# Last head's score bounds and causal mask accumulated by TensorE, with small jobs spaced wider and the transposes of two tiles re-placed, in an eight-core transformer layer

## What is computed

```
h   = layernorm(x)
q,k,v = h @ q_w.T, h @ k_w.T, h @ v_w.T          # 16 heads of 128
s   = where(causal, q @ k.T / sqrt(128), -1e30)
av  = softmax(s) @ v
out = av * sigmoid(q @ gate_w.T + gate_b)
x   = x + layernorm(out @ o_w.T)
h2  = layernorm(x)
hdn = silu(h2 @ gate_w.T * gate_s) * (h2 @ up_w.T * up_s)   # 5632 wide
x   = x + layernorm(hdn @ down_w.T * down_s)
```

## Time and profile before

| | us |
|---|---|
| median of 3 runs | 1730.98 (1730.25 to 1880.8) |
| profiled execution, its own time | 1729.22 |
| its span, slowest core (7, role B) | 1727.6 |
| spans of role B cores (1, 3, 5, 7) | 1726.4, 1727.2, 1725.2, 1727.6 |
| spans of role A cores (0, 2, 4, 6) | 1717.3, 1718.2, 1719.9, 1718.1 |
| PE busy on core 7 | 1655.5 (96%) |
| DVE, ACT busy on core 7 | 675.1 (39%), 460.9 (27%) |

### The profile page before, as it was taken

One profiled execution on the slowest core, in us unless ns is written; L12 is line 12 of the kernel. 1 busy time (PEld: TensorE's weight loads), 2 busy tenths in 40 slices (PEclk: granted clock), 3 DMA queues, 4 the chain that ended last, 5 costly groups with the idle time before them and its releaser, 6 DMA issues.

```text
span 1727.6 us, 29344 instructions; the slowest of 8 cores (1717.3 to 1727.6 us)
## 1 busy us (share of the span) xinstructions
PE 1655.5 (96%) x11548; PEld 1047.8 (61%) x11548; DVE 675.1 (39%) x1448; ACT 460.9 (27%) x723; POOL 127.5 (7%) x245
## 2 busy tenths in 40 slices
PE   3799999999999999998899999999999999999997
PEld 2556666666666666664445555555555557888853
DVE  5845656565555556566563111111111110121135
ACT  4744444444434444444122111111111110000012
POOL 0000000000000000000001000000000021111100
PEclk9999999999999999999999999999999999999999
DMA  9732222222231313034336545445454567555557
GB/s 240 230 67 44 49 38 50 38 50 38 32 55 26 62 26 50 1 67 105 122 145 130 98 77 94 86 86 92 79 97 76 97 113 126 92 91 93 87 141 231
DMA packets 43921, 152.12 MB, mean 88 GB/s; under 512 B 5120, under 2 KB 6272, under 8 KB 39040
## 3 DMA queue, kind: packets, MB, share of 16 engines
q0 software_dynamic: 34704, 102.81, 34.8%
q1 hardware_dynamic: 9072, 47.33, 8.3%
HBM read 238.24 MB, written 14.68 MB: 146 GB/s over the span
## 4 chain that ended last, share of the span: by engine, by line
PE 87%; DVE 6%; issue 3%; ACT 3%; DVEq 0%; DMA 0%; ACTq 0%; SPq 0%
PE psum L358 86%; DVE st L388 2%; DVE psum L613 1%; PE psum L363 1%; ACT b_h1b L418 1%; ACT b_kT L475 1%; DVE b_avn L657 1%; DVE b_gat L670 0%; DVE b_xb L917 0%; DMA b_yb<-y_d 0%; ACT b_P L617 0%; DVE rc L656 0%; DVEq L1271 0%; ACT mv L371 0%; DVEq L107 0%
## 5 line engine op out<-in xcount | busy, mean ns | idle before, releaser
L358 PE MATMUL psum<-b_h2T,b_fw 128*128 128x384 bf16 (+1 forms) x2752 | 520.9, 352 | 0.0
L358 PEld LDWEIGHTS psum<-b_h2T,b_fw 128*128 128x128 bf16 x2752 | 269.3, 98 | 251.3
L358 PE MATMUL psum<-b_h1T,b_wb 128*128 128x512 bf16 (+1 forms) x1536 | 386.3, 370 | 0.4 <-DVE b_Bb L550 0.4
L617 ACT ACTIVATE b_P<-psum 128x512 bf16<-128x512 f32 (+1 forms) x368 | 218.4, 593 | 395.6 <-DVE psum L613 299.6
L613 DVE TENSOR_TENSOR psum<-psum,b_Bb 128x512 f32<-128x512 f32 (+3 forms) x512 | 251.7, 511 | 149.6 <-PE psum L358 146.1
L358 PE MATMUL psum<-b_wb,b_h1T 128*128 128x256 bf16 x2048 | 270.4, 273 | 0.0
L358 PE MATMUL psum<-b_wd,b_hdn 128*128 128x256 bf16 (+1 forms) x2156 | 268.4, 288 | 0.0
L358 PEld LDWEIGHTS psum<-b_wd,b_hdn 128*128 128x128 bf16 x2156 | 211.0, 98 | 57.2
L995 DVE SCALAR_TENSOR_TENSOR b_hdn<-psum,cf,b_sg 128x512 bf16<-128x512 f32 (+1 forms) x88 | 60.1, 684 | 465.7 <-PE psum L358 461.4
L358 PEld LDWEIGHTS psum<-b_wb,b_h1T 128*128 128x128 bf16 x2048 | 193.2, 98 | 28.5
L358 PEld LDWEIGHTS psum<-b_h1T,b_wb 128*128 128x128 bf16 x1536 | 141.6, 98 | 109.7 <-issue 0.9
(11 more groups left out here) (81 smaller groups left out, 846.5 us busy)
## 6 DMA issues: line engine op xcount, KB each, us to landing
b_fw<-wg_d POOLq DMA_DIRECT2D x43, 512.0 KB, 5.2
b_fw<-wu_d POOLq DMA_DIRECT2D x43, 512.0 KB, 6.3
b_wd<-wd_d POOLq DMA_DIRECT2D x66, 256.0 KB, 3.9
xin<-x_l SPq DMA_DIRECT2D x16, 1024.0 KB, 7.5
b_wb<-wv_d POOLq DMA_DIRECT2D x16, 512.0 KB, 7.0
b_wb<-wk_d POOLq DMA_DIRECT2D x16, 512.0 KB, 5.5
b_wb<-wq_d POOLq DMA_DIRECT2D x16, 512.0 KB, 5.0
b_xb<-x_l SPq DMA_DIRECT2D x7, 1024.0 KB, 4.8
```

Source lines behind the costliest of these rows:

```text
L358: return self.q.do("T", lambda e: e.matmul(out, lhsT, rhs, start=start, stop=stop, skip_group_check=True), waits, tok)
L617: te = q.do("S", lambda e: e.activation(p[:, 0:128 * n], self.bank(b, 128 * n), ACT.Exp, scale=CSC), [ta, self.av_tok.get(gi - PRING)])
```

## The change

Six edits, all in the same program for both roles:

1. **Last head's bounds and mask on PE.** In head 15 `scores` now accumulates three things in the bank: q·k, then cneg times absq of the same columns, then on a diagonal pair idn times tri. DVE's additions, the head's `gen_sum` matmuls and their casts are gone. ACT's exp waits for PE. The scores use banks 0 and 1 only.
2. **`gen_o` twice as wide.** It covers columns 1024 to 2047 of tile 1 in banks 6 and 7: 14 matmuls in head 14, 14 in head 15. `out_proj` does 14 matmuls less for tile 1. The work is spread over all of head 14's units.
3. **Tile's own token.** `h2_ok` is kept per tile, so that the turn of tile 0 waits for tile 0.
4. **Small jobs further apart.** `pop_small` sets `rested` to `now + 3` where it was `now + 2`.
5. **`ffn` start.** Role B has three early steps (0, 1, 2) of group 0 where it had two. The last turn stands after the matmuls of the second and before their silu (in both roles one before the last early step). A one-element Silu is issued on ACT ahead of the last scaling, so that the activation table is loaded there. The weight loads `wu 2` to `wu 4` are recorded where the new order needs them; POOL's list of loads keeps its order.
6. **Last outputs.** SP waits for the eight weight-load lanes before the last tile's four output transfers instead of after.

The core of the diff ("..." marks what is left out):

```diff
     def scores(self, gi, h, segs):
-        b = gi % 2 if h < H - 1 else (0, 1, 6)[gi % 3]
+        b = gi % 2
...
+        if h == H - 1:
+            w += [self.tok["absq", h, i] for i in range(len(r.GROUPS))]
+            parts = []
+            for j, a, z, c in segs:
+                at = slice(128 * a, 128 * z)
+                parts.append((c, z - a, kt[:, 128 * j:128 * j + 128],
+                              qt[:, at]))
+                parts.append((c, z - a, self.k["cneg"], self.absq[:, at]))
+                if r.Q0 + a == j:
+                    parts.append((c, 1, self.k["idn"], self.k["tri"]))
+                n = c + z - a
+            for i, (c, m, lhsT, rhs) in enumerate(parts):
+                t = self.mm(self.bank(b)[:, 128 * c:128 * (c + m)], lhsT, rhs,
+                            i == 0, i == len(parts) - 1, w,
+                            tok=(i == len(parts) - 1))
+            self.tok["S_mm", h] = t
+            self.exp(gi, b, n, t)
+            return
...
     def pop_small(self):
-            self.rested = self.now + 2
+            self.rested = self.now + 3
...
         if s == H - 2:
-            out.append(itertools.islice(self.o_part, 6))
-            cols += 512 * 6
+            out.append(itertools.islice(self.o_part, len(self.o_done)))
+            cols += 512 * len(self.o_done)
...
     def gen_o(self):
         for kc in self.o_done:
-            self.mm(self.bank(7)[:, :], self.gat[:, kc, 128:256],
-                    self.wo_at[kc][:, 1536:2048], kc == 0, False,
...
+            for c in (2, 3):
+                self.mm(self.bank(4 + c)[:, :], self.gat[:, kc, 128:256],
+                        self.wo_at[kc][:, 512 * c:512 * c + 512],
...
-            goal = cols * (u + 1) / (nu if h < H - 2 else 0.92 * nu)
+            goal = cols * (u + 1) / (nu if h < H - 1 else 0.92 * nu)
...
     def out_proj(self):
-                         if c < 3 or kc not in self.o_done]
+                         if c < 2 or kc not in self.o_done]
...
     def o_norm(self, t, sb, done):
         tn = self.norm(m3, [ta])
+        if t == r.NQ - 1:
+            m0 = self.k["mv"][3]
+            q.do("S", lambda e: e.activation(m0[:, 7:8], m0[:, 6:7], ACT.Silu))
...
-        self.h2_ok = th
+        self.h2_ok[t] = th
...
     def h2_turn(self, t):
-                             [self.h2_ok] + self.bf[b], tok=(k == 7))
+                             [self.h2_ok[t]] + self.bf[b], tok=(k == 7))
...
     def ffn(self):
-        early = [(i, g) for i in range(2) for g in range(ng - 1)]
-        turn_at = min(len(early), 3) - 1
+        ni = 3 if ng == 2 else 2
+        early = [(i, g) for i in range(ni) for g in range(ng - 1)]
+        turn_at = len(early) - 2
+        self.cast_to("wu", 2)
         for n, (i, g) in enumerate(early):
-            self.ffn_one(i, g)
+            ready = self.ffn_mm(i, g)
             if n == turn_at:
                 self.h2_turn(r.NQ - 1)
+            self.ffn_act(i, g, ready)
...
     def last_pass(self, bank0):
+        q.put("Y", lambda e: e.nop(), [(s, s.val) for s in q.lanes["GD"]],
+              None, 0)
         self.finish(r.NQ - 1, tp, [512, 512, 512, 512])
```

More of the change, by code:

```diff
@@ L699, in fillers @@
             out.append(self.gen_abs(nh, c))
+            if nh == H - 1:
+                continue
             if c > 0:
@@ L868, in out_proj @@
         self.xb_in, self.spill, self.h2_tr, self.h2_ev = {}, {}, {}, {}
+        self.h2_ok = {}
         mv = self.k["mv"][3]
@@ L982, in ffn_one, with ffn_act @@
             self.tok["ffn_mm", i, kind] = t
+        return out, tk
+    def ffn_act(self, i, g, ready):
+        q, r = self.q, self.r
+        a, n = r.GROUPS[g]
+        w = 128 * n
+        out, tk = ready
         k = self.n_sg
```

26 lines of the change are left out of this document (16 added, 10 removed).

## The result

The changed kernel takes 1718.3 us against 1730.6: the ratio is 0.993, with a 95% interval of 0.9901 to 0.9959. The forecast was 1719.3.

The account below looks back on a forecast made before the run. TensorE, busy 1655.5 of 1727.6 us, was taken as the bound. Role B's terms summed to -12.3 (1715.3), role A's to -4.0 (1715.9); 1715.9 + 1.6 + 1.8 gave 1719.3 us, range 1715.5 to 1725.

Parts of the forecast that it names:

- the clock at head 15 stays high: Start of head 15, role B: full clock expected as waits ahead shrink from 5.2 to 2.3 us; low clock alone priced 3.4 us.
- the start part: Prologue up to the first attention scores: the change hardly touches it, so its term was 0.
- Spacing (-4.5 for B): Bank 5 in 13 heads: transpose waits of 0.35 us for gat vanish, 4.6 us together; -4.5 in role B.
- Last two heads (-2.8 for B): First output matmul in bank 7 to the output projection: 28.2 us becomes 25.4, so -2.8 in role B.
- Turn (-2.6, A -2.5): Turn of tile 0 in the output projection: wait moves to tile 2's third bank, 4.9 us; B -2.6, A about -2.5.
- My rival for the clock: Turn of tile 0: clock holds after the idle, role A -2.3 us more, time about 1717; chance 0.07.
- Feed-forward start (-2.1): First step needing the last tile, role B: 2.11 us wait goes, covered by 32 matmuls; -2.1, down to 0 if late.
- Last outputs (-0.3): End of the kernel: eight waits of SP pass before the end; -0.3 us, between 0 and -0.8.
- Low clock or long waits at head 15 as before: Rival, start of head 15: low clock or waits stay, role B only -8.9, time 1722.1 us; chance 0.17.
- spacing only moves the wait: Rival, bank 5: the wait moves to another user of the bank; role B -7.8, time 1723.2 us; chance 0.10.
- the slow last head: Rival, last head: two banks give brief stops and 1.2 GHz throughout; time 1742.2 us, a loss; chance 0.04.
- the late table: Rival, feed-forward start: table switch or late weights eat the gain; time up to 1720.8 us; chance 0.07.

Follow-up runs that it names:

- e2: Kernel before the change with only the wider distance of small jobs (now + 3): 1724.6 us, ratio 0.9964 to the kernel before.
- e1: Changed kernel with small jobs back at the old distance (now + 2): 1725.1 us, ratio 0.997 to the kernel before.
- e4: Changed kernel with the last head's bounds and masks added by VectorE again, still two banks and the wide output product: 1724.5 us.
- e10: Kernel before with wider small-job spacing and tile 0's turned copies ahead of tile 1's second statistics: 1717.9 us, ratio 0.9929 to the kernel before.
- e3: Changed kernel with the transposes of tile 0 waiting for the scaling of tile 1 again: 1719.1 us.
- e5: Changed kernel with the early output product narrow again (bank 7 alone), 14 matmuls back in tile 1: 1713.1 us, ratio 0.9906 to the kernel before.
- e6: Changed kernel with the old start of the feed-forward part (two early steps, no Silu ahead of the last scaling): 1719.9 us.
- e7: Changed kernel with 16 matmuls whose results nothing reads added behind the transposes of tile 0: 1715.4 us.
- e8: Changed kernel with the copies of turned tile 0 recorded ahead of tile 1's second statistics: 1711.6 us, ratio 0.9893 to the kernel before.
- e9: Changed kernel with tile 0's copies ahead of tile 1's second statistics and the narrow output product: 1712.7 us, ratio 0.991 to the kernel before.

## Why the prediction came out as it did

**What failed.** The sum -12.3 came near the measured -10.6 although three of its terms for role B were wrong. First, the step that the clock at head 15 stays high "because the waits ahead of it shrink from 5.2 to 2.3 us", with the -2.8 us that it credits to the last head's accumulation and the wide output product. With the waits at 5.05 us (e2) the clock stayed high on three of four B cores, and added to the spacing these two edits gave -0.7. Second, the price of a wait at bank 5, the idle shown of 0.35 us, which makes -4.5 for the spacing: it cost 0.51, and the spacing alone gave -8.6. Third, the start part, which stood at nothing: it took 4.1 us more. The first two make the heads 2.0 us better than forecast, the third makes the start worse, and they partly cancel. That the time came within 1.0 us of the forecast is in that part luck.

**Spacing (-4.5 for B): right mechanism, term mis-sized.** The waits went and nothing took their place. But I summed idle as the view shows it, 0.35 us; each such wait cost 0.51. That is 6.6 us for 13 heads. The other 2.0 us of e2 came from the low clock at head 15. In role A I allowed +0.3. There e1's heads are within 0.2 us of the changed kernel's, but spacing alone (e2) shortened them by 1.2, nearly all of the 1.3 of the change: as in role B, the edit brings most where the others are missing.

**Last two heads (-2.8 for B): right length, wrong owner.** 25.2 us against 25.4 for the stretch. The group's wait for avn, which I kept at 1.1 us, went altogether. But the clock does not follow the size of these waits: e2 has 5.05 us of them, before 5.15, and on three B cores no low clock; e4 has far more and none. Spacing alone, to which I gave nothing here, brings 2.0 us in these heads; accumulation and the wide product add 0.7, in which the accumulation is -1.5 and the wide product +0.8. Without the spacing (before against e1) the two bring 1.5. What I charged to them was mostly a low clock that is absent with the spacing alone on most cores, and with these two edits alone on all (e1), and that partly came back in e10.

**Turn (-2.6, A -2.5): right, and it held the larger finding.** The wait moved from the transposes to the third bank as traced from the order of the instructions: 4.53 us against 4.9, then the same low clock, 2.45 us against 2.3, turn at T + 43.7 against T + 44.3. Of the measured 3.1 us the own token has 1.8 (e3), where the forecast gave it all. I wrote that the 3.0 us taken out of tile 1 "buy nothing at this place". It was worse: they stretched an idle of 1.5 us to 4.5 us, and behind 1.5 us the clock holds (e5). My rival for the clock counted only on luck after the long idle; that the width of the product itself decides whether the clock falls I had not seen. The step missed was to ask what the idle would have been with the other edits and without this one.

**Feed-forward start (-2.1): right,** 2.5 by e6, although the up weights, expected 3.2 us ahead of their use, were up to 1.0 us late on two of four B cores. The small activation made the table load where it hides: the load took 1.28 us and the activation followed 0.01 us after it, the scaling ended at 917.5 and PE turned at 917.96 without waiting. The Trainium skill (ScalarE: Activation LUTs, What ACT_TABLE_LOAD costs) gives a drain of about 1.4 us with each switch; this trace shows none. With it the scaling would have been late. In role A I missed 0.7 us of wait.

**Last outputs (-0.3):** not tried apart.

**The two roles.** I had A end last by a little (1715.9 against 1715.3). B ended last by 2.5 us in the means, since its start part took 4.1 us more, on core 3 with 7.3 us of waiting for value weights. No edit touches this part. The 105.7 us of the one execution before could be a short one, but the spans speak against that: over 34 executions of the kernel before, the B cores' spans have a mean of 1726.5 us, and in the profiled one 1726.6. For the changed kernel it is 1714.8 over three executions, against 1716.0 in the profiled one. With heads and rest as in the table that leaves, as an estimate, 105.6 us of start before and 108.6 after; for e2, over nine executions, also 108.6. So about 3 of the 4.1 us look lasting. The waits differ, too: in e2 PE waits 42 us for the normalised tiles (37 to 40 before) and not for value weights. Why an edit of order in the heads goes with a longer start stays open.

**The rivals.** "Low clock or long waits at head 15 as before" did not occur (PEclk 1.00), nor did "spacing only moves the wait" (e2), the slow last head (PEclk 1.00 from 787 to 801), or the late table. Late weights did occur on two B cores, up to 1.0 us, without eating the gain. "The clock holds after the idle" did not occur behind 4.53 us on any core. Of the signs that it named all were seen, except that the roles end within 2 us: they end 2.5 apart.

## What to carry to other kernels

Price a wait by the start of the next instruction against the pace of the one ahead, not by the idle shown: each wait at bank 5 cost 0.17 us more than it showed, which for one of 0.35 us is half as much again. Price an edit also with the others left out: what two edits both remove is easily charged to the wrong one. Before taking work out in front of an idle, look at what ends that idle: if an instruction of another engine does, shorter work only makes the idle longer, and a longer idle can cost the clock of what follows; move the instruction that ends it first. In an engine's hand-written order, a short copy that frees a bank belongs ahead of a long job whose result nobody needs yet.

## What was unexpected in the hardware

- Behind an idle of 4.53 us (after) PE ran 14 matmuls in 5.47 us instead of 3.02; behind 1.51, 0.90 and 0.62 us (e5, e7, e8) it ran at full pace. Each of these idles is the same on all eight cores to within 0.1 us, and each turn to within 0.2, but for the slow one, whose turn varies from T + 42.9 to T + 43.9. What lies between 1.5 and 4.0 us of idle no run here shows.
- A low clock came and went with waits of up to 1.74 us: 0.51 from 785 to 792 on core 7 before, 1.00 on three B cores of e2 with nearly the same waits and 0.76 on the fourth (777 to 784), 0.94 over 27 us in e10, 1.00 in e4 with much longer ones. The condition stays open.
- With the narrow product role B's heads take either 687.64 or 688.98 us, different cores in e5 and e9, nothing between. The longer time goes with a low clock behind the wait of 2.0 us (PEclk 0.76 against 1.00 in the same window of e9), though the waits and the order of instructions are the same.
